# A Mamba layer with mixture of experts on one core: state sums of four channel groups at once, another ring, another way to make the residual

## What is computed

```
attn(xn): y = layernorm(xn) * g + b
          f = mamba(y), r = mamba(y reversed in time), reversed back
          out = concat(f, r) @ combine_w.T + combine_b + xn
mamba(y): xi, z = y @ in_w.T ; xi = silu(conv4(xi) + conv_b)
          dt, B, C = xi @ x_w.T ; delta = softplus(dt @ dt_w.T + dt_b)
          h[t] = h[t-1] * exp(delta[t] * A) + delta[t] * xi[t] * B[t]     256 channels x 16 states
          y[t] = sum over states (h[t] * C[t]) + xi[t] * D ;  out = (y * silu(z)) @ out_w.T
moe(xn):  each token goes to the expert (of 8) with the largest router logit:
          (silu(xn @ gate.T) * (xn @ up.T)) @ down.T
```

## Time and profile before

| | |
|---|---|
| median of 3 runs | 963.63 us (962.39 to 965.27) |
| the profiled execution | 960.58 us, span 958.7 us |
| TensorE matmul busy | 816.3 us (85%), 3009 records |
| TensorE weight load busy | 327.2 us (34%) |
| VectorE busy | 883.0 us (92%) |
| ScalarE busy | 707.4 us (74%) |
| GpSimd busy | 801.6 us (84%) |
| mean granted TensorE clock | 0.931 of full |

### The profile page before, as it was taken

One profiled execution on the slowest core, in us unless ns is written; L12 is line 12 of the kernel. 1 busy time (PEld: TensorE's weight loads), 2 busy tenths in 40 slices (PEclk: granted clock), 3 DMA queues, 4 the chain that ended last, 5 costly groups with the idle time before them and its releaser, 6 DMA issues. The chain is left out here.

```text
span 958.7 us, 10740 instructions
## 1 busy us (share of the span) xinstructions
PE 816.3 (85%) x3009; PEld 327.2 (34%) x3009; DVE 883.0 (92%) x628; ACT 707.4 (74%) x1184; POOL 801.6 (84%) x451
## 2 busy tenths in 40 slices
PE   8787887796498998989898998989989899889577
PEld 5323322141133533435233443434434242223122
DVE  4979989998899999999899899998999999998986
ACT  4588774765468899887888889898788968574540
POOL 0468676999999999988798979998798999999993
PEclk9979989898799999999799999989999998889788
DMA  6676254332364647364453655654365444553300
GB/s 210 178 213 160 50 145 97 138 102 70 129 152 154 154 125 184 98 191 116 151 130 102 188 133 173 162 157 103 86 203 133 136 105 130 133 172 74 91 0 12
DMA packets 91452, 125.56 MB, mean 131 GB/s; under 512 B 8057, under 2 KB 62714, under 8 KB 87426
## 3 DMA queue, kind: packets, MB, share of 16 engines
q1 hardware_dynamic: 89346, 120.68, 46.0%
q0 software_dynamic: 2048, 4.20, 1.3%
HBM read 77.53 MB, written 14.29 MB: 96 GB/s over the span
## 5 line engine op out<-in xcount | busy, mean ns | idle before, releaser
L1314 POOL TENSOR_TENSOR hs<-hs,C_rep 128x1024 f32<-128x1024 f32 x250 | 585.0, 2359 | 70.6 <-DVE hs L1116 37.7
L1097 DVE TENSOR_TENSOR in_b<-in_b,B_rep 128x1024 f32<-128x1024 f32 x256 | 300.3, 1217 | 41.2 <-PE in_b L580 41.0
L917 ACT ACTIVATE dA<-delta_rep,A_sb 128x511 f32<-128x511 f32 x512 | 332.9, 713 | 1.7 <-DVE hs L1116 1.2
L604 PE MATMUL y<-hs,cst 128*32 128x512 f32 x1024 | 274.1, 656 | 32.2 <-POOL hs L1314 20.8
L1116 DVE TENSOR_TENSOR_SCAN hs<-dA,in_b 128x1024 f32<-128x1024 f32 x128 | 285.5, 2268 | 8.6 <-ACT dA L917 4.8
L1114 DVE TENSOR_TENSOR_SCAN hs<-dA,in_b 128x1024 f32<-128x1024 f32 x128 | 285.2, 2268 | 2.4 <-PE y L604 1.6
L580 PE MATMUL in_b<-du,cst 128*128 128x512 f32 x256 | 144.2, 646 | 29.8 <-DVE hs L1116 20.5
L604 PEld LDWEIGHTS y<-hs,cst 128*32 128x32 f32 x1024 | 52.5, 115 | 207.1 <-issue 165.5
L541 PE MATMUL front<-xpad,w_in 128*128 128x512 f32 x248 | 120.5, 610 | 2.4 <-ACT xpad L829 1.6
L926 ACT ACT_TABLE_LOAD x71 | 91.1, 1283 | 7.3 <-PE moe L732 4.7
L580 PEld LDWEIGHTS in_b<-du,cst 128*128 128x128 f32 x256 | 43.8, 197 | 96.4 <-issue 93.7
(11 more groups left out here) (144 smaller groups left out, 805.4 us busy)
## 6 DMA issues: line engine op xcount, KB each, us to landing
delta_rep<-tmpA SPq DMA_DIRECT2D x126, 256.0 KB, 4.4
C_rep<-dbc_scratch SPq DMA_DIRECT2D x16, 1024.0 KB, 7.4
B_rep<-dbc_scratch SPq DMA_DIRECT2D x15, 1024.0 KB, 5.2
gu_w<-in_gate_up SPq DMA_DIRECT2D x39, 384.0 KB, 3.3
dn_w<-in_down SPq DMA_DIRECT2D x39, 192.0 KB, 2.5
xs<-sorted_tokens SPq DMA_DIRECT2D x39, 64.0 KB, 3.9
sorted_ffn<-ys SPq DMA_DIRECT2D x39, 64.0 KB, 2.2
sorted_tokens<-up_f SPq DMA_DIRECT2D x9, 256.0 KB, 4.5
```

Source lines behind the costliest of these rows:

```text
L604: i = e.matmul(Y[c * DD:(c + 1) * DD, :], sel, hs[:, (m + 2 * w + rh) % NH, r * L:(r + 1) * L], start=False, stop=(rh == 1 and r == RH - 1 ...
L917: i = e.activation(dA[:, m // 2 % NA, r * L + 1:(r + 1) * L], src, ACT.Exp, scale=A_sb[:, d, 2 * p + jj, r:r + 1])
L1097: e.tensor_tensor(to, in_b[:, 2 + 2 * odd, :].unsqueeze(1).broadcast_to([P, RH, L]), by, ALU.mult).then_inc(dve_mult, 1)
L1314: e.tensor_tensor(hs[:, m % NH, :], hs[:, m % NH, :], C_rep[:, u % 2, RH * rh:RH * rh + RH, :].rearrange("p r t -> p (r t)"), ALU.mult).th ...
```

## The change

1. `sum_states(u, h, rh)` handles one half rh of all four groups of a channel half: 8 matmuls over four 32-partition parts of `Y`, at steps 12 (rh 0) and 13 (rh 1) after the channel half's first step, then every 8 steps. At the end of the program the last four groups are split as before.
2. `hs` gets 13 slots (`NH`); `scan` waits for the sum call that read state m - 13.
3. `dA` has 4 slots of one half each; `decay(m)` waits for `scan(m - 4)`. `delta_rep` has 5 slots of one group (`NR`).
4. The residual: `xn_in`, its DMA and its matmul are gone. ScalarE scales x in place with `residual(b)`, by 1 + the root and the shift that it has from the layernorm, four activations for a sequence, one step ahead of `bias_mm`; one `residual_mm` follows `bias_mm`.
5. One more product with C on VectorE (step 180); 10 instead of 14 records of idle matmuls before the loop.
6. Other steps and another order inside a step, on all engines: on TensorE in_proj, turn_x, the sum call of rh 0 and x_proj now stand ahead of the spread, and z_proj stands last; on ScalarE dbc_out and dt_out come first, decay stands ahead of softplus, next_y behind it. SyncE's loads of `delta_rep` come later.

```diff
-NP = 3
-NA, NH = 3, 10
+NP, NR = 3, 5
+NA, NH = 4, 13
-C_ON_DVE = (41, 56, 217, 226, LAST - 2, LAST - 1)
+C_ON_DVE = (41, 56, 180, 217, 226, LAST - 2, LAST - 1)
...
             def load_pair(v, p):
-                if q >= NP:
-                    e.wait_ge(act_decay, 4 * (q - NP) + 4)
                 for j in range(2):
+                    if 2 * q + j >= NR:
+                        e.wait_ge(act_decay, 2 * (2 * q + j - NR) + 2)
...
-                        e.dma_start(xn_in[:, :, :], by_batch(xn_d, b)).then_inc(in_base, 16)
...
-            def sum_states(u, p, rh, groups=(0, 1)):
-
-                m = NSTEP * u + 4 * p
-                if m and p % 2 == 0 and rh == 0:
-                    e.wait_ge(act_D, 2 * u + p // 2)
+            def sum_states(u, h, rh, groups=(0, 1, 2, 3), signal=True):
+
+                m = NSTEP * u + 8 * h
+                if m and groups[0] == 0 and rh == 0:
+                    e.wait_ge(act_D, 2 * u + h)
                 wait_c(e, m + 2 * groups[-1] + rh)
                 for r in range(RH):
-                    for w in groups:
-                        c = (2 * p + w) % 4
-                        i = e.matmul(Y[c * DD:(c + 1) * DD, :], sel, hs[:, (m + 2 * w + rh) % NH, r * L:(r + 1) * L],
+                    for c in groups:
+                        i = e.matmul(Y[c * DD:(c + 1) * DD, :], sel, hs[:, (m + 2 * c + rh) % NH, r * L:(r + 1) * L],
...
             for m in range(STEPS):
                 u, s = divmod(m, NSTEP)
...
+                if m >= 12 and m - 12 < LAST - 8 and (m - 12) % 8 == 0:
+                    u2, s2 = divmod(m - 12, NSTEP)
+                    sum_states(u2, s2 // 8, 0)
+                for v in fronts(m, -11, -11):
+                    x_proj(v)
                 if m % 2 and m + 1 < LAST:
                     v, k = divmod(m + 1, NSTEP)
                     spread_du(v, k // 2)
-                for v in fronts(m, -11, -11):
-                    x_proj(v)
...
-                if m >= 8 and m - 8 < LAST - 4 and (m - 8) % 4 == 0:
-                    u2, s2 = divmod(m - 8, NSTEP)
-                    sum_states(u2, s2 // 4, 0)
...
+                if m >= 13 and m - 13 < LAST - 8 and (m - 13) % 8 == 0:
+                    u2, s2 = divmod(m - 13, NSTEP)
+                    sum_states(u2, s2 // 8, 1)
...
+            def residual(b):
...
+                for k in range(KB):
+                    o = e.activation(x_in[:, k, :], x_in[:, k, :], ACT.Identity, scale=root1[:, b, k:k + 1],
+                                     bias=shift[:, b, 0, k:k + 1])
+                o.then_inc(act_base, 1)
...
             def decay(m):
-                if m >= 2 * NA:
-                    e.wait_ge(dve_scan, m - 2 * NA + 1)
+                if m >= NA:
+                    e.wait_ge(dve_scan, m - NA + 1)
...
             def scan(m):
                 if m >= NH:
-                    e.wait_ge(pe_y, (m - NH) // 4 + 1)
+                    e.wait_ge(pe_y, (m - NH) // 8 * 2 + (m - NH) % 2 + 1)
```

More of the change, by code:

```diff
@@ L779, in tensor_program @@
                     e.transpose(M[:, IFP:IFP + P], xs[:, 0, :], ident).then_inc(pe_xs, 1)
+                for v in fronts(m, -8, -8):
+                    z_proj(v, 0)
+                for v in fronts(m, -7, -7):
+                    z_proj(v, 1)
         def scalar_program(e):
@@ L1022, in scalar_program @@
                         silu(v)
-                if m % 8 == 6 and 0 <= m // 8 - 1 < 2 * UNITS - 1:
-                    next_y(m // 8 - 1)
+                if m + LEAD < LAST:
+                    table(EXP_SET)
+                    decay(m + LEAD)
+                for b in turns(m, -19):
+                    norm_two(b)
+                for c in norms(m, 1):
+                    norm_one(c)
                 for v in fronts(m, -6, -6):
@@ L1027, in scalar_program @@
                     softplus(v, 1)
+                for v in fronts(m, -8, -9):
+                    table(EXP_SET)
+                    softplus(v, 0)
+                if m % 8 == 6 and 0 <= m // 8 - 1 < 2 * UNITS - 1:
+                    next_y(m // 8 - 1)
+                for b in gathers(m, 7):
+                    if b < NB - LATE:
+                        e.wait_ge(pe_fin, b + 1)
+                        e.copy(attn_in[:, b % 2, :, :].rearrange("p k h -> p (k h)"), M[:, :]).then_inc(act_fin, 1)
                 for b in range(NB):
```

242 lines of the change are left out of this document (115 added, 127 removed).

## The result

The changed kernel takes 937.54 us (median of 4 runs, 935.65 to 937.88) against 963.23 us of the kernel before on the same chip (962.39 to 965.27): 25.7 us less, ratio 0.9736 with a 95% interval of 0.9706 to 0.9767. The forecast was 951, its range 935 to 967. The profiled execution took 937.88 us, its span is 935.0; against the 960.58 of before that is 22.7 us less, since the profile of before lies 3 us under its median.

The account below looks back on a forecast made before the run. VectorE was taken as the bound, so only its waits, some 51 us, could be won. The terms sum to -12.7: 960.58 us profiled becomes 947.9, plus 3.05 to the median gives 951 us, range 935 to 967.

Parts of the forecast that it names:

- A sum call of 1.91 us: On TensorE, eight matmuls over four groups take 1.91 us, as four do today; 137 us leave TensorE.
- Step 10: VectorE's nine waits for the spread behind sum call and z_proj, 11.6 us: the call goes, -6.3 and -2.4.
- Step 14: Even units, six waits for the spread, 12.6 us together: one residual matmul less in TensorE's chain, -5.6.
- Residual: Identity matmuls leave TensorE before late spreads: -5.6, -0.9 and -1.9; ScalarE's 13 us of activations lie beside other work.
- , -1.9: Single 4.86 us wait of VectorE, TensorE at half clock after waiting for GpSimd's product: the residual matmul there goes, -1.9.
- Ring of 13, -2.6: VectorE's 5.2 us of waits for hs slots: half go, since a slot has more time; bounds 0 and -5.2.
- Decays, 0: Four half decays in place of three pairs: ScalarE still decays two steps ahead, no cost; bounds 0 and +5.
- Moved steps, +2.7: Spread behind in_proj and x_proj: six of 15 units would wait, 5.4 us; half taken, +2.7.
- Clock, +2.8: Middle of the run: a less busy TensorE gets granted clock 0.90, so tight spreads cost +2.8; bounds 0 and 6.
- TensorE leaving the path: Rival: with 15% of TensorE's time free, lateness no longer adds up from spread to spread; 936 us, chance 0.2.
- The rival on the slower side: Step 5 of every unit: spread queued behind x_proj, SiLU 2.5 us later, ten units wait; 974 us, chance 0.14.
- four are not side by side: Rival: a sum call takes 3.8 us, delaying spreads at step 14 and x_proj; 978 us, chance 0.03.

Follow-up runs that it names:

- e4: Kernel before with only the new parts (four-group sums, both rings, residual), all engines in the old order and steps, spread first in its step: 967.86 us.
- e12: Changed kernel with all of TensorE's list of the kernel before: 945.22 us.
- e3: Changed kernel with the spread first in its step again, as in the kernel before: 948.35 us.
- e9: e8 with the residual of before (second DMA and second identity matmul, no scaling by ScalarE): 974.41 us.
- e8: Changed kernel with 12 slots of hs in place of 13: 967.34 us.
- e6: Changed kernel with each four-group sum call made two calls of four matmuls, one after the other, no more than two groups side by side: 966.89 us.
- e7: Changed kernel with ScalarE's order inside a step, and its steps, of the kernel before: 948.68 us.
- e5: Changed kernel without the product with C on VectorE at step 180: 937.77 us.
- e14: Changed kernel with GpSimd's list of the kernel before alone: 950.03 us.
- e13: Changed kernel with SyncE's steps of the kernel before alone (loads of delta_rep and gathers): 947.90 us.
- e11: e4 with ScalarE's and TensorE's lists of the changed kernel; SyncE, GpSimd and the other steps as before: 956.37 us.
- v2: Changed kernel with two more products with C on VectorE (steps 47 and 51) and the spread first in its step for the first 16 steps: 931.89 us.
- e15: Changed kernel with the old step numbers alone (normalisation, output, no C product at 180, more idle matmuls before the loop): 933.84 us.

## Why the prediction was right and wrong

The direction and the range held; the gain was twice what was forecast (13 us of it were missing). Several sizes of the sum came out, some of them by luck. By its own steps:

- **A sum call of 1.91 us: right.** 1.92 (the row at 313.87), L602 halved to 140.9. By the Trainium skill's factor for tiles side by side ("TensorE: Matmul & The Clock Gate", section "Measured speedup vs the span model") a call would have taken some 0.3 us more, an estimate; the trace shows no such loss.
- **Step 10, 11.6 us to 2.9: the right number by luck.** 1.46 (at 307.31) + 1.36 (at 631.62) = 2.8 are left. But the sum call that leaves this chain does not bring it: it is gone in e4, e12 and e3 too, and there step 10 has 21.8, 11.6 and 10.7 us. The order of the lists decides it: at 411.86 in e3 z_proj stands ahead of the spread and waits for ScalarE's `dt_out`.
- **Step 14, 12.6 to 7.0: right in kind, too small.** Three of the waits are left, 1.10 + 0.63 + 1.00 = 2.7. I had taken each place's wait as given and only its own chain as shorter. Without the moves (e4) they are 5.7, with TensorE's old list (e12) 7.4, near the forecast: the other 4 us belong to the moves.
- **Residual, all terms together 8.4 us: the size came out, the path did not.** e9 against e8 gives 7.1, through slots and not through the spread.
- **, -1.9: about right.** 4.86 us before; 1.83 (for a slot) + 0.65 = 2.5 now.
- **Ring of 13, -2.6: wrong sign.** Slots cost 11.2 us, 6.0 more than before. The sentence that a slot has more time was true of the number of slots, not of the call: it needs the products of four groups and frees all its slots at once, and GpSimd is behind from 200 to 300 us. The call itself is then at half clock (3.64 us after 9.62 us of idle time). e8 shows how tight the ring is, and e6 that a longer call costs most of its time there.
- **Decays, 0: wrong.** The list of waits has lost all 5.6 us. ScalarE now waits 78.8 us in all before its decays, so it is ahead of VectorE; e7, ScalarE's old list, brings 3.6 back. The bound (0 to +5) left no room for a gain, though 4.8 us of waits for decays stood in the earlier trace rows.
- **C on VectorE, +1.5: harmless.** e5 shows no difference.
- **Moved steps, +2.7: the step that failed.** The only price I saw was the spread behind x_proj, and it came out by accident. In unit 0 VectorE waits 4.42 us at 59.39 and waited 1.71 before, 2.7 more, as the pattern of the earlier trace rows had given; but with the spread first again (e3) it still waits 3.66 there, so the place of the spread makes 0.8 of it. And I counted only the instructions that the spread is moved behind, not those that are moved ahead of it. e3 alone gives the position 11 us of gain, e7 ScalarE's list 11, e14 GpSimd's 12.5, e13 SyncE's 10. The prediction put all of them into one sentence ("in_proj is done earlier and so is SiLU").
- **Clock, +2.8.** The level was right (0.91 from 500 to 600), but TensorE's busy time came out at 727 in place of 670, since most of what TensorE does got longer: spreads 144.2 to 163.0 us, z_proj 35.5 to 49.0. What this cost in time was not tried apart.
- **The sign "wait for the spread near 25" did not follow from the sum.** Its own terms leave 41.0 - 8.7 - 5.6 - 0.9 - 1.9 + 2.7 + 2.8 = 29.4; 20.3 were measured.

How large the miss is, e4 shows. Without the moves and the product at step 180 the prediction's terms give 951 - 2.7 - 1.5 = 947 us; e4, which is just that, took 968. The moves were put at 2.7 us of cost and are worth 30 of gain (968 to 937.5). So the sum had 21 us too much for the parts and 33 too little for the moves, and that it ended only 13 us off is these two errors set against each other. A smaller piece of the 13 is the step from profile to median: the 3.05 us that were added have no counterpart after the change, whose profiled execution (937.88) is as long as its median.

The nearest rival, TensorE leaving the path (936), has the right number for a reason that the runs refute. In e4 TensorE is nearly as light as in the changed kernel (743.7 us) and the kernel is slower than before, with 48.1 us of waits for the spread. In the changed kernel it still has 20.3. What brought the 25 us is that the lists of four engines fit each other: the parts in the old order give 968, the new order with the old sums 957, both together 937.5. The effects are not additive. ScalarE's list is worth nothing over e4 and 11 us inside the changed kernel; setting back one of the four lists costs 8 to 12.5 us each, 42 together, where all at once, with the numbers of steps, cost 30.

The rival on the slower side was a real mechanism, though hardly of this kernel: it stands in e11 at 516.41 (3.42 us behind x_proj at half clock), which has the same TensorE list but the old lists of GpSimd and SyncE. The rival "four are not side by side" had 27 us for a call of 3.8, all of it at spreads; e6 gives 29 for 3.89, 24 of it at ring slots.

What stays open: how the gains of the lists split over single moves, and whether v2 with the step numbers of e15 would be faster still. Neither was tried.

## What to carry to other kernels

With engines that work through lists in order, price a moved instruction from both sides: what it now waits behind, and what no longer waits behind it. An instruction that waits for the bottleneck engine was best placed here after what is ready in its step (11 us), though not in unit 0, where what stood ahead of it was late itself. Take work off an engine and look what it does with the time: if it idles before the same wait, the work was not on the path, and the granted clock may take back more than was won. When buffers are freed in larger groups, count the slots for the last product of the group, not the mean.
